# Cross-attention keys of the first groups projected and placed one stage earlier, and late weights issued by POOL's queue

## The chip, the core and the metric

The kernel runs on one core of a Trainium2 chip. A core has a matrix engine (PE; PEld is its weight load), a vector engine (DVE), a scalar engine (ACT), GpSimd (POOL), a sync engine (SP) whose queue only issues transfers and waits here, and 16 DMA engines that every queue shares. The metric is the device time of one execution in microseconds (us), as a median over runs.

## What is computed

A batch of 128 sequences of 64 tokens, 128 channels each, goes through four cross-attention layers against one context tensor, each followed by another kind of feed-forward layer:

```python
x = x + xattn_L0(ln(x), ctx); x = x + low_rank_experts(ln(x))
x = x + xattn_L1(ln(x), ctx); x = x + mixture_of_16_experts(ln(x))
x = x + xattn_L2(ln(x), ctx, mask); x = x + channel_mix(ln(x))
x = x + xattn_L3(ln(x), ctx, mask); x = x + two_local_attention_and_mlp_layers(ln(x))
```

A cross-attention has 16 heads of 8 channels: `q = x Wq`, `k = ctx Wk`, `v = ctx Wv`, a softmax of `q k^T` over the 64 context tokens of the sequence, the weighted values, and an output projection. L2 has no `Wq`, `Wk`, `Wv` (queries, keys and values are the inputs themselves) and a mask for each sequence, which is loaded. Everything is float32. L3's keys and queries have a bias, L1's and L3's values too.

## The kernel before

`x` stays on chip for the whole program. Its 8192 tokens are 64 tiles of 128 tokens, worked on in 16 groups of 4 tiles (512 tokens). Each layer is a stage with its own block of instructions for each engine, written out by hand; a block ends when all engines have ended their part, and only then does any engine begin the next. `run_pipeline` runs a stage as a software pipeline: calls with g = -2 and g = -1 fill it, then come the groups, with work on groups g, g+1 and g+2 in one call.

**Keys in a cross-attention.** The scores of a tile need the keys of each head in rows of their own, with zeros around them, so that two matmuls of 64 rows cover eight heads each. The way to that layout is long: SP loads 512 context tokens (`load`, L562) into `ci`; PE projects them into the bank `ps_pj` (`project_k`, L820); ACT copies them to `k_t` (`keys`, L729 or L731); SP issues 16 transfers from `k_t`, one for each head, into the zeroed buffer `kblk` (`place_keys`, L593). In L2 the 16 transfers take their rows from `ci`. `kblk` and `ci` have two buffers each, by the parity of the group. SP issues in order: in `body(g)` first the load, in L2 then four mask loads (L571), then the 16 placements of group g+2.

**PE's order** in the first calls is: `project_k(0)`, transposes of group 0's normalised x (`transpose_x`, L472, into the same bank `ps_pj`), `project_q(0)` (L832), `project_v(0)` (L840, 32 matmul instructions), then the scores of the first tile of group 0 (L864 or L860 for a mask, L871), which wait for the placed keys; then `project_k(1)`, and the scores, transposed probabilities (L882) and weighted values (L904) of the tiles. In L1 and L3 a bias is made first (L964, L965 on PE, L810 on ACT), and PE waits for it.

**The start of every stage** from L0 on: DVE makes the variances of all 64 tiles (L391 to L397), ACT the roots (L403, L405), DVE a Newton step (L411 to L414), and then the normalised x of group 0 (L424), which PE transposes. `kblk` is written by cross-attentions alone between the program's start and the end of L3. `wide` is a list of six 512-column halves of the three buffers `probs` and `probs_t`; the stages between use at most halves 0 to 4.

**The opening block** loads x in four parts (L248), then two mask halves and the four L0 weights (L250), and then all 49 other weights and biases of the program (`late_loads`, L253); all of it is issued by SP. DVE zeroes `kblk` and takes the statistics of x (L269), and casts four small constants at its end (L275, L276). POOL draws constants. The late weights are first read after L0, in the block after `wait_for_late_loads`. POOL has no work in L0 (it has one addition for each group in L1 and L3).

Of the kernel before, what the change touches and what calls it, by code (L numbers as in the profile page):

```python
# [29 lines left out]
GTOK = GT * P  # L30
GSEQ = GTOK // S
HEADS = 16
# [22 lines left out]
gated_v biased fetched qk_copied p_scaled bias_added a_in_psum added blended bn_done c_loaded chain damped exp_ready expo_ready g_in_psum gated  # L55
# [30 lines left out]
def build_program(nc, w, x_in, ctx_t, mask_l2, mask_l3, out):  # L86

    with ExitStack() as ctx:
# [127 lines left out]
        loads += [(attn_w[n][:, :], w[n]) for n in attn_w if n.startswith("L0")]  # L216
# [26 lines left out]

        with nc.Block() as block:
            @block.sync
            def _(sp):
                for part_, s in zip(x_chunks, x_loaded):
                    sp.dma_start(x[:, part_, :], x_in[:, part_, :]).then_inc(s.sem, 16)  # L248
                for dst, src in loads:
                    sp.dma_start(dst, src).then_inc(loaded.sem, 16)  # L250
                sp.wait_ge(zeroed.sem, len(row_bias) + 3)
                for dst, src in late_loads:
                    sp.dma_start(dst, src).then_inc(loaded_late.sem, 16)  # L253
                sp.wait_ge(loaded.sem, 16 * len(loads))

# [66 lines left out]
        carried.closes(GROUPS)  # L322
        sp_turn = signal("sp_turn")
# [181 lines left out]
        def cross_attention(name, scale, mask=None, mask_per_seq=None, project=True, relu=False):  # L505
# [41 lines left out]
            value_weights = wv[:, :].rearrange("p (r j d) -> p r j d", j=2, d=HD)  # L547

# [3 lines left out]
            with nc.Block() as block:  # L552
                @block.sync
                def _(sp):
# [50 lines left out]
                @block.gpsimd  # L605
                def _(pool):
                    if bv is None:
                        return

                    def body(g, par):  # L610
                        pool.wait_ge(x_norm_ready.sem, x_norm_ready.at(g, GT))
                        pool.sem_inc(pool_turn.sem, 1)
                        rows = x[:, bass.ds(g * GT, GT), :]
                        pool.tensor_tensor(rows, rows, out_bias[name][:, :].unsqueeze(1).broadcast_to([P, GT, P]),  # L614
                                           ALU.add).then_inc(bias_added.sem, 1)

                    pool.wait_ge(bias_made.sem, 3)
                    run_pipeline(pool, body, 0)
# [101 lines left out]
                def _(act):  # L720
                    act.preload_act_table_set(LN_EXP)

                    def keys(g):
                        if not project:
# [89 lines left out]
                def _(pe):  # L814
                    def project_k(g, par):
                        wait_past(pe, v_even, g, 0)
# [236 lines left out]
        def low_rank_experts():  # L1053
# [12 lines left out]

            with nc.Block() as block:
                @block.tensor
                def _(pe):
# [37 lines left out]

                    turn_and_route(0, 0, True)
# [4 lines left out]
                def _(act):  # L1113
# [21 lines left out]
                    all_roots(act)  # L1135
                    copy_x_transposed(act, 0, 0, None, 0)
# [81 lines left out]
        def mixture():  # L1218
# [23 lines left out]

            with nc.Block() as block:
                @block.tensor
# [210 lines left out]
        def channel_mix():  # L1455
# [3 lines left out]
            k_in_psum = signal("k_in_psum", 1)  # L1459
# [15 lines left out]

            with nc.Block() as block:
                @block.tensor
                def _(pe):
# [39 lines left out]

                    pe.wait_ge(mix_ready.sem, 8)
# [3 lines left out]
                def _(act):  # L1523
                    all_roots(act)
                    act.preload_act_table_set("sigmoid_and_others")
# [713 lines left out]
        cross_attention("L0", 1.0 / np.sqrt(HD))  # L2239
# [101 lines left out]
```

## Time and profile before

| | |
|---|---|
| median of 3 runs | 3454.64 us (3454.24 to 3457.28) |
| the profiled execution's own time | 3454.24 us |
| its span in the trace | 3452.6 us |
| PE, DVE, ACT, POOL busy | 88%, 77%, 47%, 26% of the span |
| opening block, then L0, low-rank | 0 to 33.36, to 352.88, to 513.30 us |
| L1, mixture, L2, channel mix, L3 | to 834.14, to 1246.02, to 1592.08, to 1686.19, to about 2008 us |

The stage limits are the starts of DVE's first instruction in each stage (L391). PE is busy most of the time, but its busy time is that of matmuls in a pipeline, at either level of its clock, and says little about how close it is to its peak. What a few late instructions cost is read at the seams between the stages, where all engines begin together.

### The profile page before, as it was taken

The page shows a single profiled execution, that of the slowest core. Times are in us where ns is not written, and L with a number is a line of the kernel's source. Part 1 is how long each engine was busy: PE and PEld are TensorE (multiplying, and loading weights), DVE is VectorE, ACT ScalarE, POOL GpSimd, SP SyncE. Part 2 cuts the span into 40 slices and gives each one's busy share as a digit, 9 for nine tenths or more (in the row PEclk, how much of TensorE's full clock was granted, in tenths as well). Part 3 has the DMA queues.
Part 4 walks back from the last instruction along what each step waited for, and adds up shares of the span by engine and source line. Part 5 has one row for each costly group of instructions (what it writes and reads, how often), then busy time and mean ns, then how long its engine had stood idle before and what let it go on. Part 6 is the DMA issues. An engine that isn't in the chain of part 4 may idle for free. (4 is left out here: it accounts for less than half of the span.)

```text
span 3452.6 us, 95073 instructions
## 1 busy us (share of the span) xinstructions
PE 3039.5 (88%) x34096; PEld 2055.4 (60%) x34128; DVE 2674.7 (77%) x5823; ACT 1624.8 (47%) x2545; POOL 895.3 (26%) x940
## 2 busy tenths in 40 slices
PE   4999668998999979998799938898889888888889
PEld 2666555665666646666566626666655465656655
DVE  5887776886777757776588859999986599899965
ACT  2665214654333335553356625555553355555533
POOL 1000000000000000000100036666652266666634
PEclk9999668998999989999899969999999999999999
DMA  4111001110000011110011110000001100000022
GB/s 141 30 29 22 0 3 29 29 29 10 1 0 0 0 29 41 40 38 2 16 27 29 28 58 11 8 7 9 6 4 32 23 11 8 11 8 11 2 70 76
DMA packets 193348, 80.30 MB, mean 23 GB/s; under 512 B 179155, under 2 KB 182149, under 8 KB 192517
## 3 DMA queue, kind: packets, MB, share of 16 engines
q1 hardware_dynamic: 191876, 73.38, 9.1%
q0 software_dynamic: 1280, 4.20, 0.3%
q8 instruction: 142, 2.33, 0.3%
q14 instruction: 50, 0.40, 0.0%
HBM read 35.71 MB, written 8.39 MB: 13 GB/s over the span
## 5 line engine op out<-in xcount | busy, mean ns | idle before, releaser
L768 ACT ACTIVATE probs_t<-ps_pt 128x1024 f32<-128x1024 f32 x256 | 262.2, 1024 | 385.5 <-PE ps_pt L882 385.5
L630 DVE TENSOR_REDUCE row_max<-ps_s 128x16 f32<-128x1024 f32 x256 | 313.1, 1223 | 135.4 <-PE ps_s L871 132.4
L1970 POOL TENSOR_TENSOR kblk<-kblk 128x1024 f32<-128x1024 f32 x128 | 301.5, 2356 | 191.1 <-DVE kblk L2011 191.1
L635 DVE TENSOR_TENSOR probs<-ps_s,row_max 128x1024 f32<-128x1024 f32 x256 | 311.9, 1218 | 11.7
L614 POOL TENSOR_TENSOR x<-x,out_bias_L 128x512 f32 (+1 forms) x32 | 40.7, 1271 | 1028.4 <-DVE x_norm L424 519.8
L904 PE MATMUL ps_o<-v,probs_t 128*64 128x18 f32 x8192 | 285.1, 212 | 5.4 <-issue 5.2
L904 PEld LDWEIGHTS ps_o<-v,probs_t 128*64 128x64 f32 x8192 | 259.7, 138 | 40.3 <-issue 18.8
L882 PE MATMUL ps_pt<-ident,probs 128*128 128x128 f32 x2048 | 277.1, 278 | 3.1 <-ACT probs L763 3.1
L871 PE MATMUL ps_s<-kblk,q_t 64*64 64x512 f32 x2048 | 271.7, 603 | 7.0 <-issue 7.0
L763 ACT ACTIVATE probs<-probs 128x1024 f32<-128x1024 f32 x256 | 269.7, 1053 | 15.6 <-DVE probs L635 14.1
L1988 POOL TENSOR_TENSOR kblk<-kblk,small_d 128x1024 f32<-128x1024 f32 x128 | 243.6, 1903 | 50.6 <-POOL small_d L1980 50.6
L882 PEld LDWEIGHTS ps_pt<-ident,probs 128*128 128x128 f32 x2048 | 223.1, 141 | 36.7 <-issue 23.8
L1560 POOL TENSOR_TENSOR probs<-probs 128x512 f32<-128x512 f32 x16 | 16.8, 1048 | 866.6 <-ACT probs L1537 866.6
L2018 DVE TENSOR_TENSOR kblk<-ps_s,rot 128x512 f32<-128x512 f32 x256 | 173.5, 679 | 31.7 <-ACT probs L1907 31.6
L1325 ACT ACTIVATE probs<-ps_s 128x512 f32<-128x512 f32 x128 | 76.5, 597 | 226.3 <-PE ps_pt L1272 170.7
L2026 DVE TENSOR_SCALAR small_b<-small_a 128x16 f32<-128x16 f32 x128 | 169.7, 1326 | 15.0
L1817 PE MATMUL ps_s<-ident,kblk 128*128 128x128 f32 x1024 | 139.3, 280 | 38.2 <-POOL kblk L1988 37.1
L1926 ACT ACTIVATE big_flat<-ps_s 128x1024 f32<-128x1024 f32 x128 | 131.3, 1026 | 82.0 <-PE ps_s L1817 82.0
L1907 ACT ACTIVATE probs<-ps_s 128x1024 f32<-128x1024 f32 x128 | 131.0, 1024 | 79.4 <-PE ps_s L1797 75.1
L1869 PE MATMUL ps_pj<-w_lo,big_flat 128*128 128x128 f32 x1024 | 138.8, 279 | 32.1 <-ACT big_flat L1940 32.1
L1281 PEld LDWEIGHTS ps_o<-w,probs 128*128 128x128 f32 x1024 | 133.0, 191 | 49.5 <-issue 25.5
L891 PEld LDWEIGHTS ps_pt<-ident,o 128*128 128x128 f32 x256 | 35.4, 138 | 212.1 <-issue 123.3
(305 smaller groups left out, 6879.2 us busy)
## 6 DMA issues: line engine op xcount, KB each, us to landing
ci<-in_ctx_t SPq DMA_DIRECT2D x64, 256.0 KB, 3.0
kblk<-k_t SPq DMA_DIRECT2D x768, 16.0 KB
ci<-x SPq DMA_DIRECT2D x64, 128.0 KB
ci<-x SPq DMA_DIRECT2D x128, 63.0 KB
x<-in_x_in SPq DMA_DIRECT2D x4, 1024.0 KB, 8.1
mask<-in_mask_l SPq DMA_DIRECT2D x64, 64.0 KB, 2.5
kblk<-ci SPq DMA_DIRECT2D x256, 16.0 KB
out<-x SPq DMA_DIRECT2D x1, 4096.0 KB, 11.1
```

Of the source, the lines that this page charges most:

```text
L630: dve.tensor_reduce(row_max[u % 2][:, :], scores_of(u), AX, ALU.max).then_inc(max_ready.sem, 1)
L635: dve.tensor_tensor(probs[u % 2][:, :, :], scores_of(u), row_max[u % 2][:, :].unsqueeze(2).broadcast_to([P, HEADS, S]), ALU.subtract).then ...
L763: act.activation(p, p, ACT.Exp, scale=scale).then_inc(exp_ready.sem, 1)
L768: act.activation(probs_t[:, :, :], ps_pt[:, :, :].rearrange("p a (r t) -> p (a r) t", t=P), ACT.Copy).then_inc(pt_ready.sem, 1)
L871: last = pe.matmul(bank[b * S:(b + 1) * S, c, :], q_t[par][rows, tok], kblk[par][rows, :, tok], start=plain, stop=True, skip_group_check=n ...
L882: last = pe.transpose(ps_pt[:, r // 4, (r % 4) * P:(r % 4 + 1) * P], flat[:, r * P:(r + 1) * P], ident[:, :])
L904: last = pe.matmul(accumulated[half, 2 * r:2 * r + 2, :], probs_t[:, r, half], v2[par][:, 2 * u + b, r, :, :], start=True, stop=True)
L1817: last = pe.transpose(bank_ts[:, i, r * P:(r + 1) * P], rotated_qk[t % 2][:, i * INNER + r * P:i * INNER + (r + 1) * P], ident[:, :])
L1970: pool.tensor_tensor(a, a, b_, ALU.add).then_inc(rotated.sem, 1)
L1988: pool.tensor_tensor(a, a, nroot.unsqueeze(2).broadcast_to([P, 2 * LHEADS, LD]), ALU.mult)\
L2018: dve.tensor_tensor(b_[:, :, :, to:to + HALF], by_half(bank_qk)[:, :, :, of:of + HALF], table(1, to, HALF), ALU.mult).then_inc(products.se ...
L2026: dve.tensor_scalar(nrm, nwork, 1e-24, float(2 ** LOG_SCALE), ALU.max, ALU.mult)\
```

## The change

The keys of the first two groups of L1, L2 and L3, and of the first group of L0, are loaded, projected and placed in the stage before. A new class `KeysAhead` does it. Its `load` brings the context of those groups into two spaces that the earlier stage leaves unused (the sixth half of `wide`, and `x_norm_t`). `project` makes one matmul for each group, `copy` copies it back into the same space, and `place` issues 16 transfers for each. In L2 nothing is projected: the context itself is placed. `in_advance(g)` makes the cross-attention skip the projection, the copy and the placement of those groups. The loads of `ci` remain, since the values need them. PE and ACT have the projection and the copies in front of their other work of the earlier stage (in the channel mix ahead of ACT's table load too), and PE doesn't go on before the two banks are free (`banks_free`). In the opening block L0's key weight and the context of group 0 are loaded ahead of x, and the block's SP part ends with the 16 placements. The 49 late loads are issued by POOL in L0's block. Two signals have another name or base for this.

```diff
-        loads += [(attn_w[n][:, :], w[n]) for n in attn_w if n.startswith("L0")]
+        loads += [(attn_w[n][:, :], w[n]) for n in attn_w if n.startswith("L0") and n != "L0_k"]
...
+        class KeysAhead:
+            def __init__(self, name, groups=2, project=True):
+                self.name, self.groups, self.projects = name, groups, project
+                self.room = [wide[5], x_norm_t[:, :]][0:groups]
+                self.bank = [ps_pj[:, :], ps_o[:, :]][0:groups]
...
+            def load(self, sp):
+                for i, room in enumerate(self.room):
+                    sp.dma_start(room, ctx_t[:, i * GTOK:(i + 1) * GTOK]).then_inc(self.read.sem, 16)
+            def project(self, pe):
+                if not self.projects:
+                    return
+                pe.wait_ge(self.read.sem, 16 * self.groups)
+                for room, bank in zip(self.room, self.bank):
+                    pe.matmul(bank, attn_w[self.name + "_k"][:, :], room, start=True, stop=True)\
+                      .then_inc(self.in_psum.sem, 1)
...
+                for i, (room, bank) in enumerate(zip(self.room, self.bank)):
+                    act.wait_ge(self.in_psum.sem, self.in_psum.base + i + 1)
...
+                        act.activation(room, bank, ACT.Copy).then_inc(self.copied.sem, 1)
...
+            def banks_free(self, pe):
+                if self.projects:
+                    pe.wait_ge(self.copied.sem, self.copied.base + self.groups)
+            def place(self, sp):
...
+                for i, room in enumerate(self.room):
+                    if self.projects:
+                        sp.wait_ge(self.copied.sem, self.copied.base + i + 1)
+                    if i:
+                        sp.wait_ge(self.placed.sem, self.placed.base + 16 * HEADS)
+                    for h in range(HEADS):
+                        rows = slice(h * HD, (h + 1) * HD)
+                        sp.dma_start(kblk[i][rows, h % RH, :], room[rows]).then_inc(self.placed.sem, 16)
+                sp.wait_ge(self.placed.sem, self.placed.base + 16 * HEADS * self.groups)
...
             def _(sp):
+                sp.dma_start(attn_w["L0_k"][:, :], w["L0_k"]).then_inc(key_weight.sem, 16)
+                keys_ahead.load(sp)
                 for part_, s in zip(x_chunks, x_loaded):
                     sp.dma_start(x[:, part_, :], x_in[:, part_, :]).then_inc(s.sem, 16)
                 for dst, src in loads:
                     sp.dma_start(dst, src).then_inc(loaded.sem, 16)
-                sp.wait_ge(zeroed.sem, len(row_bias) + 3)
-                for dst, src in late_loads:
-                    sp.dma_start(dst, src).then_inc(loaded_late.sem, 16)
+                sp.wait_ge(blanked[0].sem, 4)
+                keys_ahead.place(sp)
                 sp.wait_ge(loaded.sem, 16 * len(loads))
...
+            def in_advance(g):
+                return isinstance(g, int) and g < ahead
...
                             load(g + 2, par)
-                            place_keys(g + 2, par)
+                            if not in_advance(g + 2):
+                                place_keys(g + 2, par)
...
                 def _(pool):
+                    if name == "L0":
+                        for dst, src in late_loads:
+                            pool.dma_start(dst, src).then_inc(loaded_late.sem, 16)
...
                     def project_k(g, par):
+                        if in_advance(g):
+                            return
...
+                    keys_ahead.project(pe)
+                    keys_ahead.banks_free(pe)
                     turn_and_route(0, 0, True)
...
                     all_roots(act)
+                    keys_ahead.copy(act)
...
-        cross_attention("L0", 1.0 / np.sqrt(HD))
+        cross_attention("L0", 1.0 / np.sqrt(HD), ahead=1)
```

PE at the seam of the low-rank experts and L1, before: the first four rows open the low-rank stage (line numbers are those of the kernel before), the others open L1.

```order
L472 MATMUL ps_pj<-ident,x_norm 128x128 x4
L1078 MATMUL ps_pt<-w_route,q_t 128x51 x4
L472 MATMUL ps_pj<-ident,x_norm 128x128 x4
L1078 MATMUL ps_pt<-w_route,q_t 128x51 x4
...
L964 MATMUL ps_o<-w_L_o,o 128x128
L965 MATMUL ps_o<-b_L_o,ones 128x128
L820 MATMUL ps_pj<-ci,w_L_k 128x512
L472 MATMUL ps_pj<-ident,x_norm 128x128 x4
L832 MATMUL ps_pj<-x_norm_t,w_L_q 128x512
L840 MATMUL ps_pj<-w_L_v,ci 64x64 x16
L864 MATMUL ps_s<-mask_L,ident 64x512 x4
L871 MATMUL ps_s<-kblk,q_t 64x512 x4
L820 MATMUL ps_pj<-ci,w_L_k 128x512
```

The same places of the changed program (with its own line numbers; L263 is `KeysAhead.project`, L540 the transposes).

```order
L263 MATMUL ps_pj<-probs_t,w_L_k 128x512
L263 MATMUL ps_o<-x_norm_t,w_L_k 128x512
L540 MATMUL ps_pj<-ident,x_norm 128x128 x4
L1161 MATMUL ps_pt<-w_route,q_t 128x51 x4
...
L1041 MATMUL ps_o<-w_L_o,o 128x128
L1042 MATMUL ps_o<-b_L_o,ones 128x128
L540 MATMUL ps_pj<-ident,x_norm 128x128 x4
L909 MATMUL ps_pj<-x_norm_t,w_L_q 128x512
L917 MATMUL ps_pj<-w_L_v,ci 64x64 x16
L941 MATMUL ps_s<-mask_L,ident 64x512 x4
L948 MATMUL ps_s<-kblk,q_t 64x512 x4
```

Two key projections have moved from L1 to the head of the stage before it, ahead of that stage's first transposes. In L1 nothing stands any longer between the bias and the transposes.

SP in the opening of L2, before: loads of the context, of four mask parts, and the 16 placements, for groups 0 and 1.

```order
L562 DMA ci<-in_ctx_t 128x8x64
L571 DMA mask<-in_mask_l 64x4x64 x4
L593 DMA kblk<-ci 8x8x64 x16
L562 DMA ci<-in_ctx_t 128x8x64
L571 DMA mask<-in_mask_l 64x4x64 x4
L593 DMA kblk<-ci 8x8x64 x16
```

And in the changed program: the mixture's stage (rows up to the first "...") now has the placements, L2's opening only the loads of the groups 0 to 2.

```order
L256 DMA probs_t<-in_ctx_t 128x512
L256 DMA x_norm_t<-in_ctx_t 128x512
L291 DMA kblk<-probs_t 8x512 x16
L291 DMA kblk<-x_norm_t 8x512 x16
...
L633 DMA ci<-in_ctx_t 128x8x64
L642 DMA mask<-in_mask_l 64x4x64 x4
L633 DMA ci<-in_ctx_t 128x8x64
L642 DMA mask<-in_mask_l 64x4x64 x4
L633 DMA ci<-in_ctx_t 128x8x64
L642 DMA mask<-in_mask_l 64x4x64 x4
L664 DMA kblk<-ci 8x8x64 x16
```

## Rows read from the trace of the kernel before

**Rows 1.** Busy time of L0 and of the low-rank stage
```profile
core 0: us, PE busy (x) PEld busy (x) DVE busy (x) ACT busy (x) POOL busy (x), PEclk, DMA share, GB/s
33.36:352.88 319.52, 292.30 (x3912) 197.74 (x3912) 243.63 (x490) 180.59 (x264) 0.00 (x0) 0.99 0.14 31
352.88:513.30 160.42, 107.62 (x512) 93.24 (x512) 121.52 (x587) 29.07 (x84) 0.00 (x0) 0.64 0.00 0
```

**Rows 2.** Timeline of the opening block (start us, us, ... [idle before <-releaser])
```profile
4.91 3.47 DVE L242 MEMSET kblk<- 128x4096 f32 x1 [0.92 <-DVE v L240]
6.44 0.45 SPq L253 DMA_DIRECT2D w_L_q<-in_L_q  x1
8.30 12.41 DVE L269 BATCH_NORM_STATS2 stats_all<-x 128x6 f32<-128x128 f32 x64
21.13 0.69 DVE L276 CAST pick_expert<-probs 128x1024 bf16<-128x1024 f32 x1
32.43 0.43 SPq L253 DMA_DIRECT2D ln_gb<-in_ln  x1
33.36 0.27 DVE L391 TENSOR_TENSOR mean_all<-stats_all 128x64 f32<-128x64 f32 x1 [11.54 <-PEq L244]
```

**Rows 3.** Timeline, opening of the first cross-attention
```profile
36.90 1.11 DVE L424 TENSOR_SCALAR x_norm<-x,mean_all,rstd_all 128x128 f32<-128x128 f32 x4
42.04 1.11 PE L472 MATMUL ps_pj<-ident,x_norm 128*128 128x128 f32 x4 [0.69 <-ACT k_t L729]
42.15 11.34 SPq L593 DMA_DIRECT2D kblk<-k_t  x16
46.70 1.97 PE L840 MATMUL ps_pj<-w_L_v,ci 128*64 128x64 f32 x32 [0.78 <-ACT q_t L755]
54.92 1.99 PE L871 MATMUL ps_s<-kblk,q_t 64*64 64x512 f32 x8 [6.26 <-issue]
56.84 2.08 PE L820 MATMUL ps_pj<-ci,w_L_k 128*128 128x512 f32 x2
71.82 1.09 PE L871 MATMUL ps_s<-kblk,q_t 64*64 64x512 f32 x8 [0.74 <-issue]
```

**Rows 4.** Timeline, opening of the second cross-attention
```profile
518.39 0.28 ACT L810 ACTIVATE out_bias_L<-ps_o 128x128 f32<-128x128 f32 x1 [2.65 <-PE ps_o L965]
521.48 1.12 PE L472 MATMUL ps_pj<-ident,x_norm 128*128 128x128 f32 x4 [0.69 <-ACT k_t L729]
533.72 0.64 PE L864 MATMUL ps_s<-mask_L,ident 64*64 64x512 bf16 x4 [5.60 <-issue]
551.13 0.41 PE L864 MATMUL ps_s<-mask_L,ident 64*64 64x512 bf16 x4 [0.70 <-issue]
```

**Rows 5.** Timeline, opening of the third cross-attention
```profile
1246.70 2.73 SPq L571 DMA_DIRECT2D mask<-in_mask_l  x4
1252.63 1.98 PE L840 MATMUL ps_pj<-ident,ci 128*64 128x64 f32 x32 [0.78 <-ACT q_t L747]
1262.86 1.99 PE L860 MATMUL ps_s<-mask,ident 64*64 64x512 f32 x8 [8.26 <-issue]
```

**Rows 6.** Timeline, opening of the fourth cross-attention
```profile
1699.21 1.98 PE L840 MATMUL ps_pj<-w_L_v,ci 128*64 128x64 f32 x32 [0.87 <-ACT q_t L757]
1707.31 0.64 PE L864 MATMUL ps_s<-mask_L,ident 64*64 64x512 bf16 x4 [6.12 <-issue]
1726.37 0.41 PE L864 MATMUL ps_s<-mask_L,ident 64*64 64x512 bf16 x4 [2.34 <-issue]
```

**Rows 7.** Timeline, first transposes of the low-rank experts and of the channel mix
```profile
357.59 1.11 PE L472 MATMUL ps_pj<-ident,x_norm 128*128 128x128 f32 x4 [5.88 <-DVE x_norm L424]
1597.31 1.09 PE L472 MATMUL ps_pj<-ident,x_norm 128*128 128x128 f32 x4 [6.21 <-DVE x_norm L424]
```

**Rows 8.** POOL's issues (ns min, median, max); context loads (us to landing)
```profile
L2179 POOL DMA_DIRECT2D out<-x x16: 557/597/784, 3320.5 to 3448.5; - x16
ci<-in_ctx_t SPq DMA_DIRECT2D x64, 256.0 KB, 3.0
```

More of the change, by code:

```diff
@@ L242, in zero_keys_and_values, with copy, run @@
             eng.memset(kblk[i][:, :, :], 0.0).then_inc(blank.sem, 1)
+        class KeysAhead:
[3 more added lines that the diff above has]
+                self.bank = [ps_pj[:, :], ps_o[:, :]][0:groups]
+                self.read = signal("ctx_ahead_" + name)
+                self.in_psum, self.copied = signal("k_in_psum"), signal("kt_ready")
+                self.placed = signal("k_placed")
+            def load(self, sp):
[8 more added lines that the diff above has]
+                      .then_inc(self.in_psum.sem, 1)
+            def copy(self, act):
+                if not self.projects:
+                    return
+                bias = col_bias.get(self.name + "_k")
+                for i, (room, bank) in enumerate(zip(self.room, self.bank)):
+                    act.wait_ge(self.in_psum.sem, self.in_psum.base + i + 1)
+                    if bias is None:
+                        act.activation(room, bank, ACT.Copy).then_inc(self.copied.sem, 1)
+                    else:
+                        act.activation(room, bank, ACT.Identity, bias=bias[:, 0:1]).then_inc(self.copied.sem, 1)
+            def banks_free(self, pe):
+                if self.projects:
+                    pe.wait_ge(self.copied.sem, self.copied.base + self.groups)
+            def place(self, sp):
+                if not self.projects:
+                    sp.wait_ge(self.read.sem, 16 * self.groups)
+                for i, room in enumerate(self.room):
[7 more added lines that the diff above has]
+                sp.wait_ge(self.placed.sem, self.placed.base + 16 * HEADS * self.groups)
+            def run(self, sp):
+                self.load(sp)
+                self.place(sp)
@@ L322, in build_program @@
         carried.closes(GROUPS)
+        loaded.base = 16 * len(loads)
         sp_turn = signal("sp_turn")
@@ L503, in wait_past, with cross_attention @@
                 eng.wait_ge(s.sem, value)
-        def cross_attention(name, scale, mask=None, mask_per_seq=None, project=True, relu=False):
+        def cross_attention(name, scale, mask=None, mask_per_seq=None, project=True, relu=False, ahead=2):
             wq, wk, wv, wo = (attn_w.get(f"{name}_{n}", ident) for n in "qkvo")
@@ L1065, in low_rank_experts, with _ @@
             y_done = signal("y_done", 1)
+            keys_ahead = KeysAhead("L1")
             with nc.Block() as block:
+                @block.sync
+                def _(sp):
+                    keys_ahead.run(sp)
                 @block.tensor
@@ L1135, in _ @@
                     all_roots(act)
+                    keys_ahead.copy(act)
                     copy_x_transposed(act, 0, 0, None, 0)
@@ L1241, in mixture, with _ @@
             hid = wide[0:SLOTS]
+            keys_ahead = KeysAhead("L2", project=False)
             with nc.Block() as block:
+                @block.sync
+                def _(sp):
+                    keys_ahead.run(sp)
                 @block.tensor
@@ L1474, in channel_mix, with _ @@
                       .rearrange("p (b t) -> p b t", t=S + 1) for t in ci]
+            keys_ahead = KeysAhead("L3")
             with nc.Block() as block:
+                @block.sync
+                def _(sp):
+                    keys_ahead.run(sp)
                 @block.tensor
@@ L1524, in _ @@
                     all_roots(act)
+                    keys_ahead.copy(act)
                     act.preload_act_table_set("sigmoid_and_others")
```

17 lines of the change are left out of this document (14 added, 3 removed).

## The prediction

> **What bounds the kernel now.** I read the busy time by stage first. In L0 PE is busy 292.3 of 319.5 us and DVE 243.6; in the low-rank stage PE is busy 107.6 of 160.4 us, at a mean granted clock of 0.64, while DVE has 121.5 [rows 1]. The middle of each stage is a full pipeline, and there the change leaves every instruction where it was. So nothing is to be looked for in it; the seams are what counts. The timelines of the seams show two things.
>
> First, in the opening block DVE is done at 21.13 + 0.69 = 21.82 us, but L0 begins only at 33.36 [rows 2]. In between SP issues late loads, 49 of them, from 6.44 to 32.86. The block ends with its slowest engine, and that is SP: 11.5 us in which no other engine works.
>
> Second, each cross-attention opens with an idle PE. In L0 the values' projection ends at 46.70 + 1.97 = 48.67, and the first scores run at 54.92, after 6.26 us of idle time whose releaser the profile doesn't name ("issue") [rows 3]. It can be worked out: SP starts the 16 placements at 42.15 and needs 11.34 us, to 53.49, and the scores start 1.43 us later. That is the landing of the last one. L1, L2 and L3 have the same hole: 5.60, 8.26 and 6.12 us [rows 4 to 6].
>
> **The opening block.** It loses the 49 issues and gains two at its head and 16 at its end. The 16 wait for the zeroed `kblk`, at 4.91 + 3.47 = 8.38 [rows 2], and for the projected keys. A context load lands 3.0 us after its issue [rows 8], and the projection costs 2.08 us at PE's low level [rows 3], so the keys are there by about 8 us too. From 8.4 us, 11.34 us of issue and 1.43 of landing give 21.2 us. DVE's 21.82 then ends the block: its 12.41 us of statistics begin as soon as the memset ends, so x two issues later costs it little. With the 0.50 us that the seam takes now (32.86 to 33.36) L0 starts at about 22.3: **-11.0 us**. The cover is thin, 0.6 us: if the placements queue behind the 4 MB of x, each us more is lost. Bounds: -8.5 to -11.1.
>
> **L0.** Placing group 0 falls out. The transposes follow the normalised x, ready at 36.90 + 1.11 = 38.01, that is 4.65 us into the stage. From transposes to the end of the values it takes 48.67 - 42.04 = 6.63 us [rows 3], unchanged. The scores then start some 11.4 us into the stage, where it was 54.92 - 33.36 = 21.6: **-10.1 us**. Group 1's keys are still made here. Its scores start 16.9 us after group 0's and wait 0.74 us [rows 3], so that chain (projection, copy, 11 us of placement) sets them, and moves along as it is. PE now runs without a hole from the values into this projection, which could take 1 us off. Against it stand the late loads, now competing for the DMA engines with the placements of groups 1 and 2. POOL's own issues take 0.60 us [rows 8], 49 of them 29 us, from 22.3 to about 52; POOL has nothing else to do [rows 1], and the loads are not needed for 290 us. In the kernel before, the placements ran at 11.34 us right behind these loads. I take +0.5, with -1 and +4 as bounds. L0 and its opening: **-20.6**.
>
> **L1.** In the stage itself the projection and the copy go too. The transposes can follow the bias, at 518.39 + 0.28 + 0.05 = 518.72 instead of 521.48, the values end 6.63 later, at 525.35, and the scores start at about 525.4 instead of 533.72 [rows 4]: -8.3. Group 1's scores wait 0.70 us, which goes with its placement: -0.5 of it, since DVE is close behind. The price stands in the low-rank stage. There PE's first transposes run at 357.59, 4.7 us after the stage's start at 352.88 [rows 1, 7]. Now they wait for two context loads (second issue some 0.5 us in, 3.0 to land, up to 0.6 for its bytes), two projections of 2.08 us and a copy of 0.6: 4.1 + 4.2 + 0.7 = 9.0 us, so +4.3. Whatever follows waits for this chain, DVE too, which has no other work there. Part of it comes back if PE's clock rises. In L0 the eight score matmuls took 1.99 us at the opening and 1.09 later, once PE had worked through scores and projection without a hole [rows 3]; the first transposes (1.11 us) and the route matmuls would shrink likewise, by up to 1.9 us. I take half of it: +3.3, bounds 2.2 and 4.3. L1 nets **-5.5**.
>
> **L2.** The mixture pays nothing: only SP, idle there, issues. In L2 the scores can follow the values at 1252.63 + 1.98 = 1254.61 instead of 1262.86 [rows 5]: **-8.1**. The cover behind is the mask: four loads issued by 1249.43, landed before 1252.5 by the 3.0 us of a context load. SP's next groups also come earlier, since 32 issues have left its queue.
>
> **L3.** The scores start at 1707.31, the values end at 1701.19 [rows 6]; that is 6.1, and 2.8 more come from the missing projection, as in L1: -8.9. Group 1's scores wait 2.34 us for their placement [rows 6], of which I take -2.0. The channel mix pays as the low-rank stage does: transposes at 1597.31 [rows 7], 5.2 us into the stage, would start 9.1 in, +3.9, and ACT's table load now stands behind the copies. A risen clock gives back more here, since two key matmul pairs follow. I take +3.3 again, bounds 2 and 5. L3 nets **-7.6**.
>
> **Sum.** -20.6 - 5.5 - 8.1 - 7.6 = -41.8 us. The profiled execution took 3454.24 us, 1.6 more than its span and 0.4 below the median, so 3454.2 - 41.8 = **3412.4 us**.
>
> **A rule weighed.** The 49 issues go to POOL beside a busy DVE. In the last stage POOL issues 16 stores at 0.56 to 0.78 us each [rows 8], beside DVE at work, and none stands out; by this row POOL is done with its part at about 52 us. The Trainium skill, SBUF — State Buffer, in "SBUF: two separate sides", says that such descriptors are written by GpSimd through a port pair it shares with DVE, that one of the two blocks the other for a whole instruction, and that DVE can starve these transfers. By that rule the late loads would come later, or DVE would run slower in L0. Both are rivals below, priced from rows.
>
> **Rivals.**
> *The first keys fare worse in traffic.* With the late loads now beside L0's groups 1 and 2, and 4 MB of x ahead of the opening's placements, either may be 5 to 8 us later. For: the thin cover of 0.6 us, and scores of group 1 that already wait. Against: the pieces are small (8 rows of 512), and issue, not bytes, takes the 11 us. It gives 3417 to 3421. Chance 0.16.
> *The projections ahead cost what they save.* If PE's wait for both loads, both copies and ACT's table load add 6 or more in each of the two stages, and the clock doesn't rise, L1 and L3 together net -7 in place of -13: 3418 to 3420. Chance 0.08.
> *DVE is blocked by POOL's issues.* If every issue held DVE up for its 0.60 us, L0 would be 29 us longer: 3441. The row of 16 stores speaks against it, and many DVE instructions in L0 read PSUM. Chance 0.03.
> *The late loads become the bound; this ends on the other side.* What follows L0 waits for all 49; L0 with the small preparation behind it ended at 352.88 us [rows 1]. If DVE starved the issues, it decides from the point where they end 21 us later than that (21 is what the three later attentions save), at 374 us: (374 - 22) / 49 = 7.2 us each. At 8 us the last is issued at 414, 61 us past 353: 3454 - 21 + 61 = 3494. Even if POOL could issue only while DVE is idle (76 of 320 us [rows 1]), 29 us of issue would take some 122 and be hidden. Chance 0.02.
> *The change doesn't do what it says*: the holes are filled by another wait, of the masks, of DVE or of the normalised x, and most of the gain goes. For L0 and L2 the rows leave no such wait. 3430 to 3450. Chance 0.03, a third of it within 0.2%.
>
> **How the numbers follow.** The main case has 0.68, with the bounds of its terms 3405 to 3419: the terms won't all fall to one side. To leave out no more than 2 in 10 the range reaches into the two first rivals: 3403 to 3422. What a measurement of this kernel can tell from no change is 0.2%, 7 us. All cases but the late-load bound and the end of the last rival lie beyond it: faster 0.96, same 0.02, slower 0.02.
>
> **What would show it.** DVE's first instruction of L0 at 22 to 23 us; no PE idle time over 1 us ahead of the first scores of L0, L1, L2 and L3; those of L0 about 11.4 us after the stage's start; the low-rank stage 2 to 4 us longer than 160.4 and the channel mix likewise; the mixture as long as now; POOL's last late load issued near 52 us. The forecast is wrong if L0's group 1 waits several us for its keys, if DVE's instructions in L0 lengthen while POOL issues, or if the first transposes after the projections come later than 10 us into their stage.

## The result, and the profile after

The changed kernel takes **3421.1 us** (median of 4 executions, 3413.9 to 3423.2), the kernel before on the same chip 3455.6: a ratio of 0.9896, 95% interval 0.9879 to 0.9913. It is 34.5 us faster; 41.8 were forecast. Two later comparisons of the same kernel gave 37.0 and 35.5 us, both at the ratio 0.9896. (The ratios are those given with the runs; the quotient of two medians differs a little, here 0.9900.)

Busy time of each stage of the changed kernel, after its opening block, in the order of the program (L0, low-rank, L1, mixture, L2, channel mix, L3; L3 up to its last addition to x on DVE). The first two rows answer to [rows 1]:

```profile
core 0: us, PE busy (x) PEld busy (x) DVE busy (x) ACT busy (x) POOL busy (x), PEclk, DMA share, GB/s
22.22:340.04 317.82, 293.27 (x3910) 199.39 (x3910) 243.99 (x490) 180.16 (x263) 26.13 (x49) 0.97 0.18 45
340.04:501.02 160.98, 112.13 (x516) 95.37 (x516) 121.90 (x587) 30.05 (x86) 0.00 (x0) 0.63 0.03 7
501.02:811.82 310.80, 296.49 (x4160) 202.38 (x4160) 244.19 (x477) 179.62 (x259) 20.35 (x16) 0.98 0.13 26
811.82:1223.43 411.61, 397.25 (x1920) 253.58 (x1920) 301.91 (x892) 141.04 (x211) 0.00 (x0) 0.98 0.01 3
1223.43:1560.19 336.76, 325.45 (x4480) 217.00 (x4480) 243.14 (x476) 165.60 (x227) 0.00 (x0) 0.98 0.18 37
1560.19:1658.43 98.24, 90.49 (x772) 65.25 (x772) 59.50 (x179) 31.87 (x54) 16.66 (x16) 0.92 0.05 11
1658.43:1972.93 314.50, 299.62 (x4160) 204.47 (x4160) 244.20 (x474) 181.62 (x258) 20.34 (x16) 0.97 0.12 26
```

Before, the same stages took 319.5, 160.4, 320.8, 411.9, 346.1, 94.1 and 321.3 us, behind an opening block of 33.4. The odd one is L0: 1.7 us shorter, where 9.6 were expected. L3 is short of its 10.9 too, by 4.1; the others lie within 3 us of the forecast.

Timeline of the changed kernel, the opening block's end and the first two groups of L0. It answers to [rows 2, 3]:

```profile
21.21 0.69 DVE L343 CAST pick_expert<-probs 128x1024 bf16<-128x1024 f32 x1
22.22 0.27 DVE L459 TENSOR_TENSOR mean_all<-stats_all 128x64 f32<-128x64 f32 x1 [0.32 <-PEq L301]
33.73 1.99 PE L948 MATMUL ps_s<-kblk,q_t 64*64 64x512 f32 x8
37.91 11.42 SPq L664 DMA_DIRECT2D kblk<-k_t  x16
48.74 1.15 PE L917 MATMUL ps_pj<-w_L_v,ci 128*64 128x64 f32 x32
54.87 1.98 PE L948 MATMUL ps_s<-kblk,q_t 64*64 64x512 f32 x8 [4.97 <-issue]
```

The opening block ends with DVE, as forecast, and the first scores start 11.5 us into L0. Then comes a new hole. Group 1's keys are issued from 37.91 to 49.33, 11.4 us as ever, but the scores that need them start at 54.87: the last placement took 5.5 us to land, not 1.4, and PE stood idle for 4.97 us. What was happening then shows in the windows of 4 us over the same stretch:

```profile
38.00:42.00 4.00, 2.73 (x24) 1.49 (x20) 3.29 (x5) 2.51 (x3) 4.00 (x9) 1.00 0.95 369
46.00:50.00 4.00, 3.90 (x68) 3.08 (x64) 3.19 (x9) 2.52 (x5) 2.86 (x6) 1.00 1.03 378
50.00:54.00 4.00, 0.00 (x0) 0.00 (x0) 0.73 (x2) 1.66 (x2) 0.00 (x0) 0.93 1.02 324
54.00:58.00 4.00, 3.13 (x25) 1.33 (x26) 1.09 (x1) 0.28 (x1) 0.00 (x0) 0.50 0.57 153
58.00:62.00 4.00, 4.00 (x32) 3.42 (x31) 1.36 (x2) 0.97 (x1) 0.00 (x0) 0.50 0.00 0
```

The last two columns are the DMA engines' busy share and the rate. They are full with late loads until 54 us, although POOL issued the last of these before 50. And the idle time has a tail: the granted clock falls from 1.00 to 0.50 (from 2.4 to 1.2 GHz), and the score matmuls take 1.98 us in place of 1.09. The time from one group's values to the next group's, called a step below, is 16.9 us, then 26.9, and 17.6 to 18.2 from there on; in the kernel before, the second of these was 18.5.

The other seams, answering to [rows 4 to 7]: the first transposes of the low-rank stage and of the channel mix, and the first matmul of the scores (with the mask) of L1, L2 and L3. None of the three has a wait before it:

```profile
347.85 0.66 PE L540 MATMUL ps_pj<-ident,x_norm 128*128 128x128 f32 x4 [0.69 <-ACT x_norm_t L273]
513.01 0.64 PE L941 MATMUL ps_s<-mask_L,ident 64*64 64x512 bf16 x4
1231.95 1.99 PE L937 MATMUL ps_s<-mask,ident 64*64 64x512 f32 x8
1568.25 1.12 PE L540 MATMUL ps_pj<-ident,x_norm 128*128 128x128 f32 x4 [0.78 <-ACT x_norm_t L275]
1670.50 0.64 PE L941 MATMUL ps_s<-mask_L,ident 64*64 64x512 bf16 x4
```

Late in L3 there is a hole of the same kind, with no late load to blame. SP needed 12.3 us for the last group's placements, from 1931.50, where the groups before it took 10.7:

```profile
1946.27 0.41 PE L941 MATMUL ps_s<-mask_L,ident 64*64 64x512 bf16 x4 [1.82 <-issue]
1949.50 1.97 PE L959 MATMUL ps_pt<-ident,probs 128*128 128x128 f32 x8
```

Again 1.8 us of idle time, again half the clock behind it (the eight transposes took 1.09 us a group earlier). L3 is 5 us longer in this profile than in the two others of the same kernel. They have the slow last placements too, 11.9 and 11.6 us, and so does the kernel before (11.5), but with a wait of 0.4 us or none behind them. What slows SP there isn't known.

### The profile page after: what moved, and what is told of

It reads as the page before. It is cut to its first block and busy times, and to the rows that moved or that the text cites. A ratio compares the mean times of both kernels' runs of the same rounds, so it can differ in the third digit from the quotient of the medians.

```text
span 3421.6 us, 95094 instructions
## 1 busy us (share of the span) xinstructions
PE 3048.3 (89%) x34128; PEld 2061.4 (60%) x34128; DVE 2676.7 (78%) x5823; ACT 1626.7 (48%) x2546; POOL 922.0 (27%) x989
## 5 line engine op out<-in xcount | busy, mean ns | idle before, releaser
L710 DVE TENSOR_TENSOR probs<-ps_s,row_max 128x1024 f32<-128x1024 f32 x256 | 312.1, 1219 | 11.7
L838 ACT ACTIVATE probs<-probs 128x1024 f32<-128x1024 f32 x256 | 269.6, 1053 | 14.2 <-DVE probs L710 12.7
## 6 DMA issues: line engine op xcount, KB each, us to landing
out<-x SPq DMA_DIRECT2D x1, 4096.0 KB, 11.1
```

Source lines behind the costliest of these rows:

```text
L710: dve.tensor_tensor(probs[u % 2][:, :, :], scores_of(u), row_max[u % 2][:, :].unsqueeze(2).broadcast_to([P, HEADS, S]), ALU.subtract).then ...
L838: act.activation(p, p, ACT.Exp, scale=scale).then_inc(exp_ready.sem, 1)
```

## The experiments

I had one theory for the 8 us missing in L0, **traffic**: the placements land late while the late loads fill the DMA engines, and no group's keys have slack to absorb it. The first rivals were that only the opening is weak, and that POOL's issues cost something by themselves wherever they stand.

### Hold the loads back, or pace them

`e1_held`, the loads behind group 1's placement:

```diff
                     if name == "L0":
+                        pool.wait_ge(k_placed.sem, k_placed.at(1, 16 * HEADS))
                         for dst, src in late_loads:
```

> The changed kernel, with one wait added: POOL issues its 49 late loads in the first cross-attention only once group 1's keys are placed. Theory (traffic): the placements are slow to land whenever the late loads fill the DMA engines, and the keys have almost no slack in any group; then group 1's interval from values to values falls from 26.9 us in the changed kernel back to about 18.5, but group 2's keys now meet the traffic and its interval grows from 18.3 to about 25; the total stays within 3 us of the changed kernel's 3421. Rival (only the opening is weak, because group 1's keys are made just behind the stage's start on a cold PE): group 2 absorbs the traffic, and the total falls by 7 to 9 us, to about 3413.

Measured: 3412.6 us, ratio 0.9882 (0.9867 to 0.9897). By the time alone the rival wins. The profile says otherwise: the step from group 1 to 2 is 18.1 us and that from 2 to 3 is 26.2, and L0 is 317.7 us long, as in the changed kernel. But this profiled execution took 3420.5 us and the three others 3410.8 to 3413.2, and the changed kernel's time is that of another chip. So I ran it again beside the changed kernel, with another that holds the loads longer.

`e10_held4` is the same edit with `k_placed.at(4, ...)`.

> The changed kernel, with all 49 late loads held until group 4's keys are placed in the first cross-attention, where the pipeline has long been full. Traffic theory: the next placement (group 5's) lands late, that interval from values to values grows from 17.7 or 18.2 to about 26, the others stay, and the total is within 3 us of the changed kernel's. Rival (a full pipeline absorbs the traffic): all intervals from group 1 on are 17 to 18.5 us, and the total is 7 to 8 us less.

> The kernel with the late loads held until group 1's keys are placed, once more, now beside the changed kernel. Its first profile showed the loss moved to group 2 (26.2 us) in full, but its other executions took 8 us less than the profiled one. If the move is what always happens: within 3 us of the changed kernel, the profiled execution no longer than the others by more than 3 us. Rival (the loss is smaller, or happens in a part of the executions alone): 4 us or more under the changed kernel, with the profiled execution again the longest.

> The changed kernel itself, beside the three others on one chip: 3416 to 3421, group 1 to group 2 at 25.5 to 27 us in its profile. What is open is whether its executions without a profile pay the loss too: the paced kernel, which cannot have it, took 7.8 us less on one chip, so they should; were they free of it, this kernel would stand at 3410.

Measured on one chip: the changed kernel 3420.2, loads behind group 1 3418.1, loads behind group 4 3420.2 us. The loss goes where the loads go: the long step is 26.0 us from group 1 to 2, 25.0 from 2 to 3, or 24.7 from 5 to 6, and all others are ordinary. L0 is 317.3, 315.8 and 316.0 us long. PE's wait in `e11_held1` and in `e10_held4`:

```profile
71.23 1.09 PE L949 MATMUL ps_s<-kblk,q_t 64*64 64x512 f32 x8 [4.07 <-DMA kblk<-k_t]
```

```profile
125.66 1.09 PE L949 MATMUL ps_s<-kblk,q_t 64*64 64x512 f32 x8 [3.39 <-DMA kblk<-k_t]
```

Here the trace names the releaser: the DMA of the keys. The rival "only the opening is weak" has fallen; a full pipeline is nearly as exposed. The loss isn't the same in every execution, though: with the loads behind group 1, four of the eight executions took 3410.8 to 3413.3 us, near the paced kernel below, and what sets it isn't known.

`e2_paced` issues four loads after each group's placement:

```diff
-                        for dst, src in late_loads:
+                        for i, (dst, src) in enumerate(late_loads):
+                            if i % 4 == 0:
+                                pool.wait_ge(k_placed.sem, k_placed.at(1 + i // 4, 16 * HEADS))
                             pool.dma_start(dst, src).then_inc(loaded_late.sem, 16)
```

> The changed kernel, but POOL issues the late loads four at a time, each four once the keys of the next group (from group 1 on) are placed. Traffic theory: four loads are 2.2 us of issues and about 2.5 us of traffic, which fit into the 5 us in which SP has no placement under way; no group's placement lands late, every interval from values to values in the first cross-attention is 17 to 18.5 us, PE's clock does not fall, and the total is 7 to 9 us below the changed kernel: 3412 to 3414. Rival (the shared cost is that of POOL's descriptors on DVE or SP, whenever they are issued): the 49 issues cost the same as before, spread over the groups, and the total stays at 3418 to 3423.

> The changed kernel itself once more, so that its time stands beside the next three on one chip. If its time is what its profile shows: 3419 to 3423, with group 1's interval of 26 to 27 us in the first cross-attention. Rival (the executions without a profile meet less traffic than the profiled one, as the spread of 3414 to 3423 may say): a median of 3413 to 3418.

> The paced kernel again (four late loads after each group's placement), beside the changed kernel on the same chip. Traffic theory: 8 us less than the changed kernel, group 1's and group 2's intervals 16.9 and 18.5 us as in its first profile. Rival (most of the difference in the first comparison was the chip): within 3 us of the changed kernel.

`e5_again` is the changed kernel, `e7_paced` is `e2_paced` once more. Measured: `e2_paced` 3408.9 us (0.9871, 0.9856 to 0.9886); then on one chip the changed kernel 3417.0 and the paced one 3409.2 (0.9875). Pacing is worth 7.8 us. In the profile of `e7_paced` the same stretch reads:

```profile
38.00:42.00 4.00, 2.76 (x24) 1.62 (x26) 3.29 (x5) 2.69 (x3) 0.00 (x0) 1.00 0.11 21
46.00:50.00 4.00, 4.00 (x66) 3.11 (x66) 3.19 (x10) 2.52 (x5) 0.27 (x1) 1.00 0.26 55
50.00:54.00 4.00, 4.00 (x53) 2.66 (x45) 3.01 (x3) 2.66 (x4) 2.03 (x4) 1.00 0.41 101
```

PE works through and the clock stays up. L0 is 309.4 us long, 10.1 less than before: the very 10.1 of the forecast, without its +0.5. All 49 loads are still issued by POOL, so their issuing by itself costs nothing that the length of L0 shows. In the changed kernel itself DVE shows what the issues do to it. Its row maxima from 22 to 50 us (line, count, busy us, mean ns), first in the changed kernel, where POOL issues nearly all that time:

```profile
L705 DVE TENSOR_REDUCE row_max<-ps_s 128x16 f32<-128x1024 f32 x4 | 4.9, 1223 | 2.6 <-PE ps_s L948 2.6
```

And in the paced one, where it hardly does:

```profile
L707 DVE TENSOR_REDUCE row_max<-ps_s 128x16 f32<-128x1024 f32 x4 | 4.9, 1222 | 2.6 <-PE ps_s L950 2.6
```

1223 against 1222 ns: these weren't held up; they read PSUM. Two short DVE instructions on SBUF alone were, by a little. In the changed kernel and then in the paced one:

```profile
23.14 0.27 DVE L462 TENSOR_SCALAR mean_all<-mean_all 128x64 f32<-128x64 f32 x1
23.70 0.29 DVE L464 TENSOR_SCALAR dev_all<-dev_all 128x64 f32<-128x64 f32 x1
```

```profile
23.14 0.20 DVE L462 TENSOR_SCALAR mean_all<-mean_all 128x64 f32<-128x64 f32 x1
23.62 0.20 DVE L464 TENSOR_SCALAR dev_all<-dev_all 128x64 f32<-128x64 f32 x1
```

They take 0.27 to 0.29 us in all six profiles in which POOL issues at this time, and 0.19 to 0.20 in all others, so it is no chance, but it is 0.2 us in all. Whether POOL's work or the loads' traffic slows them, no run separates. The Trainium skill, SBUF — State Buffer, in "SBUF: two separate sides", has DVE and POOL's descriptor writes lock each other out for a whole instruction, on DVE's side only for instructions that take the port pair they share. The rows agree in so far as few DVE instructions are touched, but none waited for the whole 0.54 us of an issue.

### One part alone

`e3_loads` is the kernel before with the late loads moved to POOL's queue in L0, and nothing else:

```diff
                 for dst, src in loads:
                     sp.dma_start(dst, src).then_inc(loaded.sem, 16)
-                sp.wait_ge(zeroed.sem, len(row_bias) + 3)
-                for dst, src in late_loads:
-                    sp.dma_start(dst, src).then_inc(loaded_late.sem, 16)
...
                 def _(pool):
+                    if name == "L0":
+                        for dst, src in late_loads:
+                            pool.dma_start(dst, src).then_inc(loaded_late.sem, 16)
```

> The kernel before with only the late loads moved to POOL's queue in the first cross-attention; no keys are made ahead anywhere. Additive theory: the opening ends at about 22.2 us in place of 33.4 (11.1 us gained), and the traffic then lands on the placements of groups 0 and 1 of the first cross-attention and costs 4 to 9 us; total 3448 to 3452. Rival (the traffic costs only where keys are ahead, as group 0's keys have waited anyway): the whole 11 us shows, 3443 to 3445. From this run and the changed kernel the keys ahead alone are worth 27 to 31 us.

Measured: 3443.8 us (0.9969, 0.9959 to 0.9978), 11.2 less: by the time the rival, the opening's whole 11 us. But the profiled execution took 3453.7, and there L0 is 331.9 us, 12.4 longer than before. Two late landings make it up:

```profile
45.34 1.98 PE L871 MATMUL ps_s<-kblk,q_t 64*64 64x512 f32 x8 [10.57 <-issue]
57.74 2.05 PE L820 MATMUL ps_pj<-ci,w_L_k 128*128 128x512 f32 x2 [10.41 <-DMA ci<-in_ctx_t]
```

The keys of group 0 landed 6.2 us after their last issue, and a context load that SP issued at 39.33 held PE until 57.74, 18 us, where 3.0 is the rule [rows 8]. The nine executions without a profile (3439.5 to 3446.3) cannot have paid all this. How late a landing is in heavy traffic varies, then, from execution to execution, and what the profile itself adds to it I can't tell. This stays open; that the changed kernel pays some 8 us without a profile too is shown by the paced kernel.

`e6_L02` leaves out the keys ahead of L1 and L3. The low-rank stage and the channel mix lose their `KeysAhead` with its loads, projections, copies and placements, and:

```diff
-        cross_attention("L1", 1.0 / np.sqrt(HD), mask=masks["L1"])
+        cross_attention("L1", 1.0 / np.sqrt(HD), mask=masks["L1"], ahead=0)
...
-        cross_attention("L3", 1.0 / np.sqrt(HD), mask=masks["L3"])
+        cross_attention("L3", 1.0 / np.sqrt(HD), mask=masks["L3"], ahead=0)
```

> The changed kernel without the keys ahead of L1 and L3; those of L0 and L2 and the late loads on POOL's queue stay. By the stage lengths of the two profiles L1 and the low-rank stage together gave 9.5 us and L3 and the channel mix 2.7 us (6.8 gained, 4.1 paid), so this kernel takes 12 us more than the changed one. By the prediction's terms it would be 13.1 (5.5 and 7.6). Rival (PE's clock at the openings is chance and made L1's gain look larger and L3's smaller): 12 to 14 in total all the same, but L1 with the low-rank stage near 7 and L3 with the channel mix near 6.

Measured beside `e5_again`: 3429.7 against 3417.0, so 12.7 us, where the forecast's terms say 13.1. This agrees. Which of the two stages gives how much its profile doesn't tell: the profiled execution took 3440.7 us, 11 more than the median, and has one long step in either stage (23.7 us in L1, 22.4 in L3).

### What the projections ahead cost

`e4_later` moves them behind the first two groups' work, into banks that are free there (`ps_s` in the low-rank stage, whose edit is shown; `ps_pt` in the channel mix, likewise), and their copies with them:

```diff
-                    keys_ahead.project(pe)
-                    keys_ahead.banks_free(pe)
                     turn_and_route(0, 0, True)
                     turn_and_route(1, 1)
+                    keys_ahead.project(pe)
```

> The changed kernel, with the projections of the keys of L1 and L3 moved behind the first two groups' own work in the low-rank stage and the channel mix, into PSUM banks that those stages leave free at that time, so that nothing waits for them. Theory (the price of the projections is their place at the head of PE's order): the first transposes come back to 4.7 us and 5.2 us into their stages (now 7.8 and 8.1), the channel mix falls from 98.2 to about 94.5 us, and the low-rank stage from 161.0 to about 160.4 or stays, since PE then starts cold again; total 3416 to 3418. Rival (the extra 4 us of the channel mix come from the later ACT table load or from SP's traffic): the channel mix stays above 97 and the total at 3420 to 3422.

Measured: 3422.4 us, 0.9909 (0.9894 to 0.9924): nothing gained. The first transposes did come back to 4.7 and 5.2 us. But in the low-rank stage the projections now stood before group 0's own products, and their copies before its exponentials: the stage is 165.5 us long. The channel mix came to 97.0, not 94.5. I took the clock for what was left: it is 0.50 over the first 10 us of the channel mix in the changed kernel and here. But it is 0.50 in the kernel before as well. What differs is the second 10 us, in the kernel before and in the changed one:

```profile
1602.10:1612.10 10.00, 10.00 (x91) 7.04 (x90) 5.17 (x14) 3.47 (x6) 2.20 (x2) 1.00 0.00 1
```

```profile
1570.20:1580.20 10.00, 10.00 (x55) 6.37 (x56) 2.26 (x7) 2.39 (x4) 1.27 (x2) 0.72 0.12 23
```

PE is busy all of this time, and the stage's whole difference has arisen by the transposes of the third group: they start 15.6 us into the stage before, 19.7 in the changed kernel, 18.4 in `e4_later` and 16.5 in `e6_L02`, which has nothing ahead of L3. In the changed kernel 2.9 of the 4.1 us stand before the first key matmuls (the wait for the loads, two projections, a copy), and 1.2 behind them, where the clock rises later than before. In `e4_later` the two projections take 1.7 us of a PE that has no gap to hide them in, and the late clock the other 1.1. That the clock can rise late there without any projection, `e6_L02` shows: it loses 0.9 us so.

`e8_filled` is the paced kernel with filler matmuls in L0 to L3:

```diff
+                    def fill(n):
+                        for _ in range(n):
+                            pe.matmul(ps_pt[:, 1, 0:P], ident[:, :], ident[:, :], start=True, stop=True)
...
+                        if isinstance(g, int) and g == -1:
+                            fill(6)
...
+                    fill(12)
```

> The paced kernel, with 12 matmuls of 128x128 added at the head of PE's work in each cross-attention, where PE has nothing to do for 4 to 5 us, and 6 more in its wait for the first exponentials; their results go to a PSUM bank that nobody reads, so only their time counts. Theory (each opening runs at half TensorE clock, because PE stood idle before it, and L1's first interval of 17.0 us in the changed kernel and 21.8 us in the paced one differ by how soon the clock rises): the granted clock in the first 10 us behind the transposes rises from about 0.5 towards 1, the chain of transposes, queries, values and scores shortens by 2 to 4 us, no first interval is above 17.5 us, and four openings give 8 to 16 us: 3397 to 3404 where the paced kernel takes 3412. Rival (the clock does not rise on so little work, or what follows waits for DVE and ACT anyway): within 3 us of the paced kernel.

Measured: **3397.5 us**, 0.9836 (0.9822 to 0.9849), 11.6 under the paced kernel on the same chip. PE's first work in L0 in `e7_paced` (transposes, queries, scores), then in `e8_filled` (the 12 fillers as 24 records, transposes, queries, values, scores):

```profile
27.03 1.09 PE L540 MATMUL ps_pj<-ident,x_norm 128*128 128x128 f32 x4 [20.72 <-DVE x_norm L492]
28.80 2.07 PE L911 MATMUL ps_pj<-x_norm_t,w_L_q 128*128 128x512 f32 x2 [0.69 <-ACT x_norm_t L821]
33.56 1.99 PE L950 MATMUL ps_s<-kblk,q_t 64*64 64x512 f32 x8
```

```profile
22.22 4.84 PE L894 MATMUL ps_pt<-ident 128*128 128x128 f32 x24 [15.94 <-PEq L301]
27.03 0.63 PE L540 MATMUL ps_pj<-ident,x_norm 128*128 128x128 f32 x4
28.35 1.13 PE L915 MATMUL ps_pj<-x_norm_t,w_L_q 128*128 128x512 f32 x2 [0.69 <-ACT x_norm_t L821]
30.25 1.15 PE L923 MATMUL ps_pj<-w_L_v,ci 128*64 128x64 f32 x32 [0.78 <-ACT q_t L832]
31.34 1.09 PE L954 MATMUL ps_s<-kblk,q_t 64*64 64x512 f32 x8
```

The transposes start at the same time, 27.03, for they wait for DVE. The transposes and what follows take little over half as long, and the scores come 2.2 us sooner. The first step between groups is now 15.2 to 15.6 us in L0, L1 and L3, where it was 16.5 to 19.1 in the profiles of the changed kernel, and 21.7 in L1 of `e2_paced`. That first step is where PE's clock differed from execution to execution: in L1 the granted clock over the second 10 us was 0.84 in the changed kernel's first profile (step 17.0 us) and 0.67 in `e5_again` (19.1).

`e9_heads` adds 9 fillers ahead of the projections in the low-rank stage and the channel mix, in `project`:

```diff
+                if self.groups > 1:
+                    for _ in range(9):
+                        pe.matmul(self.bank[1][:, 0:P], ident[:, :], ident[:, :], start=True, stop=True)
                 pe.wait_ge(self.read.sem, 16 * self.groups)
```

> The kernel with pacing and fillers, with 9 more filler matmuls of 128x128 at the head of PE's work in the low-rank stage and in the channel mix, where PE waits 3.4 us for the two context loads before it projects the keys ahead. Theory (in the channel mix the projections cost 4.1 us because PE's clock stayed low there): the projections, transposes and first route or key matmuls run at the upper clock, the first transposes come 1.5 to 2 us sooner, the channel mix falls from 98 to about 96 and the low-rank stage by up to 2; total 3393 to 3396, against 3397.5. Rival (the price is the wait for the loads and the copies, which the clock does not touch): no change, 3396 to 3399.

Measured, on another chip than `e8_filled`: **3386.1 us**, 0.9801 (0.9788 to 0.9815), the fastest of all and 7 us under what was expected at best. The opening of the channel mix, first 10 us, in `e8_filled` and then in `e9_heads`, with PE's busy time and its clock (last but two):

```profile
1547.40:1557.40 10.00, 4.96 (x9) 1.96 (x9) 5.49 (x27) 3.77 (x6) 0.00 (x0) 0.50 0.20 59
```

```profile
1544.50:1554.50 10.00, 7.97 (x29) 5.78 (x30) 5.79 (x27) 3.77 (x6) 0.00 (x0) 0.78 0.20 59
```

The channel mix falls from 97.8 to 94.4 us, 0.3 above its 94.1 before the change. That is a balance of two things: the first key matmuls still start 1.7 us later than before, and what follows is 1.5 us shorter, at the full clock. A kernel with fillers and no projections was not run, so this doesn't say that the projections have become free. The low-rank stage falls from 163.7 to 161.4. Up to the start of L3 the profiles differ by 6.4 us of the 11.4. The other 5 lie behind it, above all in the two local attentions: 555 and 542 us in this profile, 543 and 561 in that of `e8_filled`, 7 less together. The edit doesn't touch them, and why they shift is open; only the 6.4 can be put down to the fillers.

## Why the prediction was right, and where its sizes were off

The time lay in the range and on the right side; the gain was forecast 7 us too large. That it lay in the range owes something to luck: the main case, 3405 to 3419, missed it, and it was the room left for the first rival, up to 3422, that held it, by 0.9 us. One sign of being wrong that the prediction named did occur: L0's group 1 waited 5 us for its keys. By its terms, with the three profiles of the changed kernel (`e5_again` and `e12_again` are the second and the third):

| term | forecast | first | second | third |
|---|---|---|---|---|
| opening block | -11.0 | -11.1 | -11.1 | -11.1 |
| L0 | -9.6 | -1.7 | -3.0 | -2.2 |
| low-rank | +3.3 | +0.6 | +2.0 | +3.5 |
| L1 | -8.8 | -10.0 | -8.3 | -8.0 |
| mixture | 0 | -0.3 | -0.3 | -0.1 |
| L2 | -8.1 | -9.3 | -9.3 | -9.3 |
| channel mix | +3.3 | +4.1 | +4.1 | +4.2 |
| L3 | -10.9 | -6.8 | -11.7 | -11.9 |
| sum | -41.8 | -34.5 | -37.7 | -35.0 |

(Each is the difference of the stage's length, from DVE's first instruction in it to that of the next; L3 to the next stage's table load on ACT. The sums are of the unrounded lengths.)

- **Opening block:** right to 0.1 us. The thin cover of 0.6 us held.
- **L0, the term that was mis-sized.** The step "Against it stand the late loads ... I take +0.5, with -1 and +4 as bounds" came to +7.1 to +8.4 in the profiles and 7.8 by the times (L0's change less the -10.1). The reason given, that in the kernel before the placements ran at 11.34 us right behind these loads, failed twice. It looked at the wrong length: the issue stayed at 11.4 us, and it was the landing behind it that went from 1.4 to 5.5. And the placements of the kernel before, from 42.15, had no such loads beside them; the share of the DMA engines had fallen to 0.02 by then (last column but one):

```profile
33.00:38.00 5.00, 0.00 (x0) 0.00 (x0) 3.61 (x15) 1.79 (x3) 0.00 (x0) 1.00 0.97 329
38.00:42.00 4.00, 2.07 (x2) 0.50 (x2) 0.01 (x1) 0.60 (x1) 0.00 (x0) 1.00 0.02 5
```

The bound of +4 missed also that 5 us without work cost PE half its clock for some 8 us more, or about 4 us of work. The first rival described this case, at 3417 to 3421, where the kernel is; it had 0.16 and deserved more. The row that spoke for it, group 1's scores waiting 0.74 us already [rows 3], meant no slack at all.
- **Low-rank stage and L1:** the mechanism is right: the wait for the loads, two projections and a copy bring the first transposes 7.8 us into the stage (9.0 forecast). In the first two profiles the clock rose there (0.66 us for the transposes, not 1.11) and gave more back than I took; in the third it did not (1.11), and the stage pays 3.5. With L1 the net is -9.5, -6.3 and -4.5 in the three profiles around the forecast -5.5. This spread goes with the clock at the two openings, and an exact term for one seam is not to be had.
- **L2:** the scores follow the values with no wait. Of the 1.2 us beyond the forecast, 0.2 is the rest of the wait of 8.26, and 0.5 comes from a clock that rises sooner without it (the first scores against keys take 1.41 us, where they took 1.96). The remaining 0.5 isn't traced.
- **Channel mix and L3:** -2.7, -7.6 and -7.7 against -7.6. The first has the hole of 1946 us in it. Of the +4.1 in the channel mix, "a risen clock gives back more here" was wrong: the clock rose later than before and took 1.2 us. The first transposes came 2.8 us later where 3.9 were forecast.
- **DVE blocked, late loads the bound:** both fell as prices. Two short DVE instructions lengthened by 0.08 to 0.09 us each, not by 0.60 an issue, and the last load was issued before 50 us, forecast 52.

## What to carry to other kernels

A small transfer that is issued just in time has two lengths, its issue and its landing, and here bulk loads on another queue stretched the landing: that the bulk is not needed for a long time is a reason to spread it over the moments without small transfers, not to send it early. Where PE waits for other engines at the head of a stage, the chain behind that wait ran at half clock here, and a few matmuls into an unused bank in that wait are cheap: they gave 11.6 us. Before a cost is put down to such a half clock, look whether the kernel before had it too.

## What the runs showed of the hardware that I had not expected

- Transfers of two queues meet: with the DMA engines at a share of 0.95 to 1.03, a 16 KB placement on SP's queue landed 5.2 to 6.2 us after its issue, in place of 1.4, and one context load took 18. The Trainium skill, DMA: Bandwidth & Descriptors, in "Queues, rings and completion order", has the queues as rows that share the same 16 engines, served in turn, a packet at a time; the late landings agree.
- The windows' granted clock did not show the cold start of L0: from 22.2 to 32.2 us it reads 1.00 in `e7_paced`, while the queries' matmul took 2.07 us, twice the 1.13 that it took in `e8_filled`. In L1 and in the channel mix it reads 0.50 beside the same durations. Where the two disagree I went by the durations.
